# Two cross-attention layers on one core: key and query stacks filled before the block boundary, and another order of layer 1

## The reference

```python
q = hidden_state @ Wq + bq                       # 4 x 512 x 512
k = encoder_hidden_state @ Wk + bk               # 4 x 1601 x 128
v = encoder_hidden_state @ Wv + bv
scores = einsum('bkgld,bksd->bkgls', q, k) * scale + encoder_attention_mask
attn = softmax(scores, axis=-1)
out = einsum('bkgls,bksd->bkgld', attn, v) @ Wo + bo
x = out + hidden_state                           # then layer norm with gamma, beta
```

## Time and profile before

| | |
|---|---|
| median of 3 runs | 4081.09 us (4077.36 to 4091.4) |
| profiled execution | 4077.36 us, of it 4075.7 us between the first and the last instruction |
| mean granted TensorE clock | 0.968 |
| PE busy | 3798.1 us, 93% |
| DVE, ACT, POOL busy | 63%, 54%, 47% |
| one batch | about 1018 us: layer 0 and the middle up to 579.7 us, layer 1 from there on |

### The profile page before, as it was taken

The page is one execution under the profiler, slowest core; times in us unless marked ns, Lnnn a source line. Parts: engine busy times, 40 slices in busy tenths (PEclk is TensorE's granted clock), DMA queues, the critical chain, the costliest instruction groups (busy, mean ns, idle before and its releaser), DMA issues. The chain is left out here.

```text
span 4075.7 us, 55973 instructions
## 1 busy us (share of the span) xinstructions
PE 3798.1 (93%) x18688; PEld 1913.5 (47%) x18688; DVE 2551.6 (63%) x6969; ACT 2209.4 (54%) x2592; POOL 1920.0 (47%) x940
## 2 busy tenths in 40 slices
PE   8999899997899989999789998999978999899997
PEld 4444664443444466444344446644424444664442
DVE  3556458885356645888535665588853566558885
ACT  0556228885055623888505561388850556238885
POOL 0667126554066712655406671265640667126554
PEclk9999989999999998999999999899989999989999
DMA  4222331110422243111042214311104222331110
GB/s 122 43 46 46 142 83 21 23 20 11 122 43 47 44 144 81 21 23 19 11 122 43 50 41 144 81 22 23 19 12 121 43 46 45 144 81 21 23 19 11
DMA packets 103874, 226.61 MB, mean 56 GB/s; under 512 B 23364, under 2 KB 44612, under 8 KB 94856
## 3 DMA queue, kind: packets, MB, share of 16 engines
q1 hardware_dynamic: 99144, 217.47, 21.9%
q10 hardware_dynamic: 4416, 5.30, 0.5%
HBM read 117.13 MB, written 4.19 MB: 30 GB/s over the span
## 5 line engine op out<-in xcount | busy, mean ns | idle before, releaser
L1155 DVE CUSTOM_DVE_ANT_0 tile_b<-l_psR,hT 128x400 f32<-128x400 f32 (+1 forms) x2048 | 1070.8, 571 | 286.6 <-PE l_psR L1229 277.8
L1092 POOL TENSOR_TENSOR l_pt<-l_pt,l_maskT 128x1024 f32<-128x1024 f32 (+1 forms) x384 | 913.2, 2391 | 601.6 <-ACT l_pt L1114 601.6
L504 DVE TENSOR_REDUCE l_acc<-l_psR 128x1 f32<-128x424 f32 (+1 forms) x1280 | 704.0, 590 | 386.7 <-PE l_psR L584 378.6
L476 ACT ACTIVATE l_pt<-l_psB 128x1024 f32<-128x1024 f32 (+1 forms) x576 | 554.0, 976 | 250.0 <-PE l_psB L606 187.4
L1229 PE MATMUL l_psR<-split_w,qst 64*128 64x400 f32 (+1 forms) x2048 | 554.7, 448 | 29.4 <-PEq L1342 12.6
L1128 ACT ACTIVATE l_pt<-l_pt 128x1024 f32<-128x1024 f32 (+1 forms) x512 | 533.5, 1056 | 49.5 <-POOL l_pt L1092 47.7
L1229 PEld LDWEIGHTS l_psR<-split_w,qst 64*128 64x128 f32 x2048 | 264.1, 191 | 505.1 <-DVE l_acc L1155 366.9
L1272 PE MATMUL l_psO<-l_pt,V 128*32 128x512 f32 (+1 forms) x3328 | 475.0, 604 | 8.2 <-ACT l_pt L1128 7.0
L584 PE MATMUL l_psR<-l_kst,l_qst 128*128 128x424 f32 (+1 forms) x1280 | 469.7, 411 | 13.0 <-DVE l_acc L504 8.5
L1255 PE MATMUL l_psB<-qst,split_w 64*128 64x512 f32 (+1 forms) x1664 | 407.1, 419 | 6.0 <-ACT l_pt L1122 2.7
L1122 ACT ACTIVATE l_pt<-l_psB 128x1024 f32<-128x1024 f32 x320 | 327.8, 1024 | 133.7 <-PE l_psB L1259 126.8
(11 more groups left out here) (143 smaller groups left out, 4429.9 us busy)
## 6 DMA issues: line engine op xcount, KB each, us to landing
l_kst<-l_khl SPq DMA_DIRECT2D x192, 264.1 KB, 3.8
mid_w<-in_w SPq DMA_DIRECT2D x128, 256.0 KB, 3.8
split_w<-k SPq DMA_DIRECT2D x192, 100.1 KB, 4.0
hT<-in_maskN SPq DMA_DIRECT2D x16, 800.5 KB, 10.9
l_qst<-l_qhl SPq DMA_DIRECT2D x192, 64.0 KB, 2.0
qst<-q SPq DMA_DIRECT2D x384, 32.0 KB
hT<-in_ctxT SPq DMA_DIRECT2D x12, 800.0 KB, 11.7
tile_c<-in_wo SPq DMA_DIRECT2D x8, 1024.0 KB, 5.9
```

The source lines that it names most:

```text
L476: act.activation(pt[0:r, n % NPT0, 0:w], psB[0:r, 2 * (n % 2):2 * (n % 2) + 2, :].rearrange("p a n -> p (a n)")[:, 0:w], ACT.Exp).then_inc ...
L504: dve.tensor_reduce(acc[:, h % 2, qt, c:c + 1], psR[:, ring[item] % NR, 0:w], AX.X, ALU.max).then_inc(s_red, 1)
L1092: pool.tensor_tensor(probabilities(n, r), probabilities(n, r), mask_of(t, r), ALU.add).then_inc(s_padd, 1)
L1155: dve.tensor_tensor_reduce(junk[:, n % 2, 0:hi - lo], bank(at)[:, 0:hi - lo], maskN[:, qt, lo:hi], 1.0, -3e38, ALU.add, ALU.max, acc[:, p ...
```

## The change

It has four parts.

1. What fills the constant rows. POOL's two memsets are gone. DVE now does all of it, behind the last additions of the MLP: rows 32 to 63 of each half of `kst` to zero and one padding column of the 32 rows above, then the two rows of ones, then rows 32 to 63 of each half of `qst` to zero. One semaphore `s_last` counts these 8 instructions. SP waits for 6 before the keys and for 8 before the queries.
2. What is copied where. SP's list in the middle block now has the keys of both slots and the queries of all four slots. The layer 1 block no longer begins with them.
3. `copy_queries` always issues 8 DMAs: the two maximum rows come from padding rows of `kst` and not from `qst`. The first A of every pair waits for 128 counts for each use of its slot, and once for `s_last`.
4. The plan. Other MASKED_BY, RANK, LENGTH, LATER, AHEAD 2 and FEW 3; the costs of a changed array layout are gone.

```diff
-MASKED_BY, LAST_BY, LAST_PAIRS = "apapadpapadpa", "apapadpapadpa", 1
+MASKED_BY, LAST_BY, LAST_PAIRS = "paapapapapaad", "paapapapapaad", 1
-RANK = {"PE": "YMaXABWO", "DVE": "NDZTR", "ACT": "JESCP", "POOL": "G"}
+RANK = {"PE": "MYXaBWAO", "DVE": "NZDTR", "ACT": "JESCP", "POOL": "G"}
-AHEAD, FEW = 1, 1
-TOGETHER, SWITCH = False, 9
+AHEAD, FEW = 2, 3
...
-                    if engine == "PE":
-                        length += SWITCH * (tiles != TILES[k])
-                        tiles = TILES["M"] if k == "B" and mode[x] == "p" else TILES[k]
-                        if k == "A" and x[3] and last == ("A", *x[:3], 0):
-                            length = 1
-                        last = (k, *x)
+                    if k == "A" and x[3] and partner == ("A", *x[:3], 0):
+                        length = 2
+                    if engine == "PE":
+                        partner = (k, *x)
...
-        sp.wait_ge(s_ones, 1)
+        sp.wait_ge(s_last, 6)
         copy_keys(sp, kst, k1, 0, s_k1)
-        sp.wait_ge(s_zeros, 1)
+        sp.wait_ge(s_last, 8)
         sp.wait_ge(s_split, kq[("Q", 0)])
-        copy_queries(sp, qst, q1, 0, s_stack)
+        for p in range(2):
+            copy_queries(sp, qst, q1, kst, p, s_stack)
+        copy_keys(sp, kst, k1, 1, s_k1)
+        for p in range(2, SLOTS):
+            copy_queries(sp, qst, q1, kst, p, s_stack)
...
-            if item == ("Q", 0):
-                pool.wait_ge(s_h, NF)
-                for i in range(2):
-                    pool.memset(kst[:, i, :].bitcast(F32), 1.0).then_inc(s_ones, 1)
...
-        dve.memset(qst[:, :, :].bitcast(F32), 0.0).then_inc(s_zeros, 1)
+        for lo in (32, 96):
+            dve.memset(kst[lo:lo + 32, :, :].bitcast(F32), 0.0).then_inc(s_last, 1)
+            dve.memset(kst[lo - 32:lo, :, N1:N1 + 1].bitcast(F32), 0.0).then_inc(s_last, 1)
+        dve.wait_ge(s_last, 4)
+        for lo in (32, 96):
+            dve.memset(kst[lo:lo + 2, :, :].bitcast(F32), 1.0).then_inc(s_last, 1)
+        for lo in (32, 96):
+            dve.memset(qst[lo:lo + 32, :, :].bitcast(F32), 0.0).then_inc(s_last, 1)
...
-        if p >= SLOTS:
-            sp.dma_start(qst[64 * e + 32:64 * e + 34, s, :].bitcast(F32),
-                         qst[64 * e + 34:64 * e + 36, s, :].bitcast(F32)).then_inc(s_stack[s], 16)
+        sp.dma_start(qst[64 * e + 32:64 * e + 34, s, :].bitcast(F32),
+                     kst[34:36, 0, 0:L].bitcast(F32)).then_inc(s_stack[s], 16)
...
-        copy_queries(sp, qst, q1, 1, s_stack)
...
-        sp.wait_ge(s_ones, 2)
-        copy_keys(sp, kst, k1, 1, s_k)
-        for p in range(2, SLOTS):
-            copy_queries(sp, qst, q1, p, s_stack)
...
-                    pe.wait_ge(s_stack[s], 128 * (p // SLOTS) + 96)
+                    pe.wait_ge(s_last, 8)
+                    pe.wait_ge(s_stack[s], 128 * (p // SLOTS + 1))
```

More of the change, by code:

```diff
@@ L62 @@
 LOWEST = -3e38
-RANK = {"PE": "YMaXABWO", "DVE": "NDZTR", "ACT": "JESCP", "POOL": "G"}
-LENGTH = {"A": 28, "T": 50, "M": 35, "B": 24, "mask": 101, "W": 91, "D": 114, "C": 94, "P": 94, "J": 103, "E": 52, "G": 234, "N": 55, "Y": 46, "S": 55, "R": 86, "X": 46, "Z": 60, "O": 260}
-LATER = {"PE": 23, "DVE": 18, "ACT": 16, "POOL": 11}
-AHEAD, FEW = 1, 1
-TOGETHER, SWITCH = False, 9
-TILES = {"A": "r", "B": "r", "M": "f", "O": "f", "W": "c", "Y": "c", "X": "c"}
+RANK = {"PE": "MYXaBWAO", "DVE": "NZDTR", "ACT": "JESCP", "POOL": "G"}
+LENGTH = {"A": 20, "T": 50, "M": 40, "B": 27, "mask": 94, "W": 102, "D": 114, "C": 94, "P": 94, "J": 103, "E": 52, "G": 234, "N": 55, "Y": 52, "S": 55, "R": 86, "X": 52, "Z": 60, "O": 260}
+LATER = {"PE": 23, "DVE": 15, "ACT": 16, "POOL": 11}
+AHEAD, FEW = 2, 3
 def rows(tile, n):
@@ L191, in plan_layer1, with bank @@
     index = {x: i for i, x in enumerate(score)}
-    now, free, ends, plan, ring, tiles, last = 0, dict.fromkeys(RANK, 0), {}, [], [], "", ("",)
+    now, free, ends, plan, ring, partner = 0, dict.fromkeys(RANK, 0), {}, [], [], None
     def done(*item):
         return ends.get(item, 1 << 30) <= now
-    def bank(ahead=0):
-        i = len(ring) + ahead - NR
-        return i < 0 or i < len(ring) and done(*ring[i])
+    def bank():
+        return len(ring) < NR or done(*ring[len(ring) - NR])
     def left(x):
@@ L213, in ready @@
         if k == "A":
-            return (x[0] < 2 or done("N", x[0] - 2)) and x[0] <= (todo["B"] or [(pairs,)])[0][0] + AHEAD \
-                and (not TOGETHER or x[3] == 1 or bank(1))
+            return (x[0] < 2 or done("N", x[0] - 2)) and x[0] <= (todo["B"] or [(pairs,)])[0][0] + AHEAD
         if k == "T":
@@ L251, in plan_layer1 @@
                     if k == "a":
-                        k = "A" if waiting < FEW or TOGETHER and last[0] == "A" and last[4] == 0 else ""
+                        k = "A" if waiting < FEW else ""
                     options = todo.get(k, [])[:12 if k == "P" else 1]
@@ L681, in middle @@
     kst, qst = key_stacks(keep["split_w"]), keep["qst"]
-    s_ones, s_zeros = sem("l1_stack_ones"), sem("l1_stack_zeros")
     hb = sb("hb", [P, 2, L])
@@ L691, in middle @@
     s_wkv, s_wo, s_x, s_c, s_wq1 = (sem("mid_" + n) for n in ("wkv1_in", "wo_in", "x_in", "bc_in", "wq1_in"))
-    s_wo1, s_mn1, s_c1 = (sem("l1_" + n) for n in ("wo_in", "maskN_in", "bc_in"))
+    s_wo1, s_mn1, s_c1, s_last = (sem("l1_" + n) for n in ("wo_in", "maskN_in", "bc_in", "last_rows"))
     s_k1 = [sem(f"l1_k_in{i}") for i in range(2)]
@@ L950, in copy_keys, with copy_queries @@
 def copy_keys(sp, kst, k1, kv, s_k):
-    for row, part in ((0, 0), (16, 1), (48, 0)):
-        for half in (0, 64):
+    for half in (0, 64):
+        for row, part in ((0, 0), (16, 1), (48, 0)):
             sp.dma_start(kst[half + row:half + row + 16, kv % 2, 0:N1].bitcast(F32),
                          k1[16 * kv:16 * kv + 16, part, :].bitcast(F32)).then_inc(s_k[kv % 2], 16)
-def copy_queries(sp, qst, q1, p, s_stack):
+def copy_queries(sp, qst, q1, kst, p, s_stack):
     s = p % SLOTS
@@ L1006, in layer1_attention @@
     s_stack = [sem(f"l1_q_in{i}") for i in range(SLOTS)]
-    s_ones = sem("l1_stack_ones")
+    s_last = sem("l1_last_rows")
     s_m = sem("l1_m_full")
@@ L1065, in _ @@
             if p + SLOTS < PAIRS_OF_HEADS:
-                copy_queries(sp, qst, q1, p + SLOTS, s_stack)
+                copy_queries(sp, qst, q1, kst, p + SLOTS, s_stack)
         for q in range(QT):
```

## The result

The changed kernel takes 4208.35 us (median of 4 runs, 4205.88 to 4211.37); the kernel before, run beside it, 4085.03. The ratio is 1.0303, 95% interval 1.0282 to 1.0325. The forecast was 4177, with 4125 to 4235 as range. The profiled execution took 4201.49 us, its span is 4199.8, 124.1 longer than before.

What follows compares the result with a forecast made beforehand. PE was taken to bound layer 1's steady pairs at 23.21 us. The profiled 4077.4 us, + 92.5 for the barrier, 0 for the plan and 4 for layer 1's end gave 4173.9; the median's 3.7 more made 4177, range 4125 to 4235.

Steps and rivals of the forecast that it cites:

- SP ends the middle block: Middle block's end: SP, issuing 44 DMAs ahead of the barrier, drains last; 23.1 us per batch, 92.5 in four.
- the copies don't hold the barrier: Rival at the middle block's end: PE starts once keys 0 and queries 0 are issued; 4094 us, chance 5%.
- SP's prices: SP's issuing ahead of the barrier: 4.4 us for six key copies, 0.65 for each query or small copy.
- The memsets on DVE: Middle block's end: eight memsets at 0.83 ns a column, count of 6 at 572.5 us, of 8 at 576.0.
- Layer 1 only shifted, and no cost of clock at its start: Start of layer 1: first A to first tile stays 21 us, and PE's longer idle costs no clock; 0 for both.
- The plan, 0 per pair: Layer 1's pairs: the new order's costs and savings sum to 0, ends -0.65 and +1.0 us per pair.
- The wait in the run of six A's: Layer 1's pairs: six A's share three banks and the last waits for DVE; +0.5 us per pair.
- -0.25 for one start less and the -0.25 for a wait that goes: Layer 1's pairs: 11 runs instead of 12, and one wait behind two DVE tiles gone; -0.25 us per pair each.
- the gain of the plan: Rival in layer 1: fewer runs and no new wait, -0.65 us per pair; 4135 us, chance 17%.
- its loss of one ACT wait a pair: Rival in layer 1: PE waits for one whole ACT operation per pair, +64 us; 4241 us, chance 17%.
- DVE really held PE: Rival in layer 1: lighter DVE lets a pair fall to ACT's 21.2 us, -128 us; 4049 us, chance 4%.
- The end of layer 1, +1 a batch: End of layer 1: four more tiles run with no A beside them; +1 us per batch, 4 in all.

Runs made afterwards that it cites:

- Experiments 3 and 4: Changed kernel with copies for slots 1 to 3 and second keys behind the barrier, 4130.08 us; kernel before with all its copies ahead of it, 4127.19 us.
- Experiment 7: Changed kernel without the eight small copies of cleared rows at each slot's first use: 4193.69 us, ratio 1.0263.
- experiment 9: Changed kernel without the small first-use copies of cleared rows and with two long DVE memsets less: 4166.00 us, ratio 1.0189.
- experiment 1: Changed kernel with the tables and planner of the kernel before, so only constant rows and copies differ from that kernel: 4193.14 us, ratio 1.0257.
- experiment 2: Kernel before with the tables and planner of the changed one, its memsets and copies kept: 4095.64 us, ratio 1.0023.
- experiments 6 and 8: Last pair's ACT and POOL tiles masked by DVE instead: in the kernel before, 4077.20 us; in that kernel with the changed planner and tables, 4091.21 us.

## Why the prediction was right, and where it was short

**SP ends the middle block: right.** This was the forecast's main step, and each of its signs came: SP's drain last (603.4, told for about 602), PE's first A at 604.24 (told 603), an idle time of PE of 29.6 us (told 26). The first two lie so near only because this batch's middle block ended 2 us earlier; the idle time shows what was missing. Experiments 3 and 4 show it from both sides: with the copies behind the barrier SP is only 6.6 us behind POOL, and with nothing but the copies moved it is 10.4 us behind it and the kernel 42 us slower. The rival "the copies don't hold the barrier" (4094) is out.

**SP's prices: right within 2%.** 44 DMAs at 4.4 per six keys and 0.65 for each other are 29.6 us; SP took 30.2, 0.6 more. Experiment 7 took eight small ones away and had 4.8 us.

**The memsets on DVE: the term that was mis-sized.** The prediction took the busy time, 0.83 ns a column, and had the count of 6 after 11.0 us and that of 8 after 14.5, counted from 561.48; from the end of the additions, 0.38 us earlier, that is 11.4 and 14.9. From there (559.05) the trace has them after 14.0 and 18.5. Counted from the start of the additions, which lies 2.05 us earlier than before, SP's last DMA was foretold at 602.2 - 558.62 = 43.6 us and its drain came at 603.4 - 556.57 = 46.8: 3.2 us a batch, 12.8 in all. Of these 2.6 a batch are the later count of 6 and 0.6 SP's own issuing; the count of 8, at 577.57, came just as SP had issued the keys and cost nothing more. That narrow memsets aren't cheaper held: 2 x 3204 takes 2.73 us as 32 x 3204 does. What was missed is the idle ahead of each, 0.72 for 3204 columns and 0.48 for 2048, which belongs to its price. Its kind stood in the row that I read for the price, as `[0.38 <-issue]`, and experiment 9 confirms it with 3.4 us a memset.

On this the Trainium skill ("VectorE: DVE Perf Modes", section "Zero memsets can be issued as uint32 (trn2)") was the better guide. Its one cycle per element at 0.96 GHz is 3.34 us for 3204 columns and 2.13 for 2048; from start to start the trace has 3.45 and 2.24. The prediction gave 9 us for this rule and put it aside for the busy time of the row.

**Layer 1 only shifted, and no cost of clock at its start: right.** From the first A to the first tile it is 625.37 - 604.24 = 21.1 us, as the 21 before. During the idle time of 29.6 us the granted clock falls, and the first A's start at the lower level, 1.2 GHz, on which this phase ran before too, from 1 us behind its first A on the earlier trace rows:

```profile
604.30:614.30 10.00, 9.55 (x21) 5.44 (x21) 9.24 (x37) 1.89 (x3) 6.42 (x6) 0.50 0.77 250
624.40:628.40 4.00, 3.53 (x10) 2.13 (x12) 2.00 (x8) 2.05 (x3) 0.00 (x0) 0.50 0.00 0
```

It is back at 1.00 within 27 us of the first A in both kernels, and experiment 1 has the long idle time in every batch and layer 1 at its old length in three of four.

**The plan, 0 per pair: too low.** The busy times were close (ACT 20.79 for 21.2, POOL 16.70 for 16.7, DVE 18.33 for 18.2), and none became the bound. The wait in the run of six A's is there too, at half its size, 0.26 us and not 0.5:

```profile
699.08 0.95 PE L1223 MATMUL l_psR<-split_w,qst 64*128 64x400 f32 x2 [0.26 <-DVE l_acc L1148]
```

Then the other side of the sum must be too large: of the -0.25 for one start less and the -0.25 for a wait that goes nearly nothing can have come, since a pair takes 0.19 us more. That is a subtraction; no run holds the two apart. Four pairs with their sums take 0.25 us more, sixteen so about 1.0, which was told as 0. By both the gain of the plan (4135) and its loss of one ACT wait a pair (4241) are out. "DVE really held PE" is out too: DVE has 1.1 us less per pair, and the loader's waits for its maxima are 12.1 us in 23 times over two pairs (671 to 718 us), for 11.1 in 18, and no pair is faster.

**The end of layer 1, +1 a batch: 1.6, and work that had been put off.** Plan and end together cost 3.6 us a batch, where 1 was told. A cut at the first tile of the last pair says where they are. It comes 379.6 us after the first A in the kernel before and in experiment 2 alike. From it to PE's last matmul, before and in experiment 2:

```profile
959.48:998.44 38.96, 35.67 (x150) 13.06 (x150) 10.14 (x13) 20.85 (x23) 14.42 (x7) 1.00 0.00 0
```

```profile
957.92:1000.42 42.50, 37.56 (x166) 13.28 (x166) 9.55 (x13) 24.58 (x27) 18.93 (x9) 1.00 0.00 1
```

Of the 3.5 us more, 1.9 are busy time, for 16 more matmuls: two bursts of W that the new order had not yet done at that point (72 matmuls of W are left and not 56). The other 1.6 are idle time (4.94 for 3.29). So the fifteen pairs ahead only seem to cost nothing; they took the same time with 1.9 us less of work done, of which the periods above show 1.0. The prediction named the later W's, but put no price on them in its sum. For the end it reckoned with four tiles without A's beside them; the order has the A's done three tiles earlier (tile 8 for tile 11), and the idle time there grew by 1.6 and not 1. With a last pair masked by DVE (experiments 6 and 8) the same cut gives 37.08 us with 35.35 busy for the old plan and 40.06 with 37.53 for the new one: there the work put off is 2.2 of 3.0 us.

**A clock that fell at the end: not foreseen.** In three of four batches of the changed kernel the stretch from the last J to the last E took 34.0 to 34.2 us, in the fourth 32.56. In the first batch, and likewise in the third, the long wait of PE is followed by this (granted clock 1.00 over the stretch in the fourth batch):

```profile
988.91 1.93 PE L1266 MATMUL l_psO<-l_pt,V 128*32 128x512 f32 x8 [2.01 <-ACT l_pt L1121]
```

```profile
984.00:989.00 5.00, 2.99 (x20) 1.16 (x24) 0.49 (x1) 4.67 (x6) 4.19 (x2) 0.98 0.00 0
989.00:994.00 5.00, 5.00 (x20) 1.56 (x20) 0.00 (x0) 3.45 (x4) 1.70 (x2) 0.68 0.00 0
```

Eight matmuls take 1.93 us and not 1.06. In the second batch the same wait passes at the full clock, and the fall comes with the next long wait, 17 us later (six matmuls in 4.49 us and not 2.81):

```profile
2040.60 1.06 PE L1266 MATMUL l_psO<-l_pt,V 128*32 128x512 f32 x8 [2.01 <-ACT l_pt L1121]
2057.22 4.49 PE L1279 MATMUL l_psB<-tile_c,attnT 128*128 128x512 f32 x6 [1.58 <-ACT l_pt L1121]
```

This is 1.5 us three times, 4.5 in all. Experiments 1, 2 and 3 had it in one batch of four, with either plan. Why it came more often in the changed kernel is open; no run here holds that apart.

**The sum.** 4173.9 for the profiled execution, + 10.4 for the memsets, + 2.4 for SP's issuing, + 10.4 for plan and end (3.6 and not 1 in four batches), + 4.5 for the clock is 4201.6; it took 4201.49. That it agrees to 0.1 is luck, since executions of one kernel lie several us apart. In differences of medians: told were 95.9 us more, measured 123.3, and the four terms are 27.7 of the 27.4 between. The median lies 31 us above the forecast and inside the range. These terms all add in one direction; only inside the plan's term did two errors offset each other, a wait of half the size and savings that didn't come.

## What to carry to other kernels

A DMA that is issued ahead of a barrier costs its issue time on the path as soon as SP is one of those that the barrier waits for; moved forward to be early, 24 copies that nobody awaited cost 10 us a batch, and 30 of them 20 us where their start was late as well. Price a repeated instruction by the distance from one start to the next, with the idle "<-issue" ahead of it, and not by its busy time. At the end of a phase give the work to the engine that has run out: masking the last pair on DVE made the kernel 0.2% faster than the one before (4077.2 us), the best version found. And an order of work is compared at a point where equally much is done: the new plan reached the last pair as early as the old one, with two bursts of W still to do.

## What the hardware showed unexpectedly

- A DVE memset of float32 takes as long on 2 partitions as on 32 (2.73 us busy for 3204 columns), and an idle of 0.22 to 0.23 ns a column stands ahead of it (0.72 and 0.48 us; 0.38 ahead of the one of 128 x 2048), also where no semaphore holds it; two memsets of 3204 columns taken away gave 6.9 us.
- One PE wait of 2.0 us at the full granted clock was followed by five microseconds at a mean of 0.68, in some batches and not in others of the same run; in one batch that wait passed at the full clock and one of 1.6 us, 17 us later, went with such a fall (0.66). Each cost about 1.5 us.
- Behind the first A of layer 1 the clock comes back to 1.00 in most batches after 24 to 27 us and in some (two of four in experiment 7) after 30 to 31, which costs up to 1.7 us.
